# Post-norm decoder layer on one core: the mixer's GpSimd order, and the products ahead of its last mix

## The reference

```python
xn = _layernorm(x, ln_gamma, ln_beta)
k = jnp.einsum('btc,dc->btd', xn, Wk)
v = jnp.einsum('btc,dc->btd', xn, Wv)
r = jnp.einsum('btc,dc->btd', xn, Wr)
kv = k * v
weighted_kv = kv * jnp.power(td[None, None, :], t_idx)
csum = jnp.cumsum(weighted_kv, axis=1)
shifted = concatenate([zeros, csum[:, :-1]], axis=1)
wkv = tf * kv + td * shifted
out = jnp.einsum('btc,dc->btd', jax.nn.sigmoid(r) * wkv, Wo)
x = _layernorm(x + out)
```

## Time and profile before

| | |
|---|---|
| median of 3 runs | 2131.97 us (2131.47 to 2137.92) |
| profiled execution | 2134.5 us, its span 2132.7 us |
| granted TensorE clock, mean | 0.975 of full speed |
| TensorE busy | 1984.1 us, 93% |
| VectorE busy | 1530.2 us, 72% |
| ScalarE busy | 1254.4 us, 59% |
| GpSimd busy | 1478.0 us, 69% |
| mixer, 14.0 to 268.7 us | TensorE busy 226.12, VectorE 205.69, GpSimd 146.75, ScalarE 131.58 us; clock 0.99 |

### The profile page before, as it was taken

One profiled execution on the slowest core, in us unless ns is written; L12 is line 12 of the kernel. 1 busy time (PEld: TensorE's weight loads), 2 busy tenths in 40 slices (PEclk: granted clock), 3 DMA queues, 4 the chain that ended last, 5 costly groups with the idle time before them and its releaser, 6 DMA issues. The chain is left out here.

```text
span 2132.7 us, 51909 instructions
## 1 busy us (share of the span) xinstructions
PE 1984.1 (93%) x14320; PEld 1787.2 (84%) x14320; DVE 1530.2 (72%) x3648; ACT 1254.4 (59%) x3478; POOL 1478.0 (69%) x1691
## 2 busy tenths in 40 slices
PE   5999879999999999785999999999999999489997
PEld 5777668888887888675999999999999999468886
DVE  5888747777787788763777778888888888335554
ACT  3555446666666666532777777777777777224443
POOL 3656512777677677663677778888888888459764
PEclk9999999999999999997999999999999999789999
DMA  3300022432422423304666766777777777367542
GB/s 122 109 0 0 0 94 80 139 101 79 158 79 90 147 79 118 110 21 139 228 230 228 232 228 227 236 237 237 237 235 229 230 233 234 110 242 241 182 168 99
DMA packets 244904, 329.89 MB, mean 155 GB/s; under 512 B 50074, under 2 KB 167234, under 8 KB 244836
## 3 DMA queue, kind: packets, MB, share of 16 engines
q1 hardware_dynamic: 218788, 279.97, 40.5%
q0 software_dynamic: 26048, 49.10, 6.3%
HBM read 236.17 MB, written 77.18 MB: 147 GB/s over the span
## 5 line engine op out<-in xcount | busy, mean ns | idle before, releaser
L1336 POOL DMA_INDIRECT slot_token<-a_entry,a_slot_i x256 | 261.4, 1021 | 113.2 <-issue 71.8
L1818 POOL DMA_INDIRECT part_rows<-e_out,e_dest x184 | 211.0, 1147 | 74.2 <-issue 65.9
L1951 ACT ACTIVATE e_sg<-e_g 128x256 f32<-128x256 f32 x368 | 141.8, 385 | 204.7 <-PE e_g L1643 204.7
L1810 POOL DMA_INDIRECT e_xg<-x_rows,e_tok x188 | 196.5, 1045 | 85.1 <-issue 56.3
L2000 DVE TENSOR_TENSOR e_h<-e_sg,e_u 128x256 f32<-128x256 f32 x368 | 158.0, 429 | 100.4 <-PE e_u L1643 40.5
L1161 ACT ACTIVATE a_prob<-a_s,a_ntop 128x128 f32<-128x128 f32 x512 | 180.8, 398 | 3.0 <-DVE a_ntop L1515 2.9
L1826 POOL TENSOR_TENSOR e_wd1l<-e_raw_d,e_wd1h 128x256 fp32r<-128x256 f32 x184 | 145.5, 825 | 19.1 <-ACT e_wd1h L1931 18.4
L1826 POOL TENSOR_TENSOR e_wd0l<-e_raw_d,e_wd0h 128x256 fp32r<-128x256 f32 x184 | 145.9, 827 | 14.4 <-ACT e_wd0h L1931 13.6
L2015 DVE TENSOR_SCALAR e_out<-e_d,e_dest 128x256 f32<-128x256 f32 x184 | 80.6, 480 | 103.1 <-PE e_d L1643 103.1
L1643 PE MATMUL e_d<-e_wd1h,e_ht1h 128*128 128x256 f32 x368 | 109.4, 297 | 24.6 <-issue 24.6
L1023 PE MATMUL a_o<-a_wo,a_ot 128*128 128x256 f32 x512 | 123.1, 384 | 8.2 <-DVE a_ot L1582 8.2
(11 more groups left out here) (398 smaller groups left out, 7603.2 us busy)
## 6 DMA issues: line engine op xcount, KB each, us to landing
e_raw_g<-in_eg SPq DMA_DIRECT2D x94, 512.0 KB
e_raw_u<-in_eu SPq DMA_DIRECT2D x94, 512.0 KB, 5.6
e_raw_d<-in_ed SPq DMA_DIRECT2D x93, 512.0 KB
part_rows<-a_zero SPq DMA_DIRECT2D x16, 2048.0 KB
f_part<-part_rows SPq DMA_DIRECT2D x16, 2048.0 KB, 9.5
x<-in_x SPq DMA_DIRECT2D x16, 512.0 KB, 3.7
x_rows<-x SPq DMA_DIRECT2D x16, 512.0 KB
out_rows<-f_res SPq DMA_DIRECT2D x16, 512.0 KB, 10.2
```

The source lines that it names most:

```text
L1336: pool.indirect_dma_start(k.slot_tok, bass.IndirectOffsetOnAxis(ap=slot_i[:, j, q:q + 1], axis=0), entry[:, j, q, :], None, bounds_check=S ...
L1810: pool.indirect_dma_start(xg[a][:, n, :], None, k.x2_d, bass.IndirectOffsetOnAxis(ap=tok[a][:, n, 0:1], axis=0))\
L1818: pool.indirect_dma_start(k.part_d, bass.IndirectOffsetOnAxis(ap=dest[a][:, n, 1:2], axis=0), out[a][:, n, :], None).then_inc(put[a], 16)
L1951: act.activation(sg[m % 2][:], bank_g[m % 2][:, 0:SETW], ACT.Silu).then_inc(sg_rdy, 1)
```

## The change

GpSimd's period puts the root behind both wkv_in, in every period, and the context's low part between the two wkv_in of the last period. At the mixer's end TensorE makes four products ahead of the last mix instead of two, and ScalarE empties all four banks before the outgoing norm of group 14.

```diff
                 periods(pe, period)
-                project_ahead(range(2))
+                project_ahead(range(4))
                 mix(NG - 1, 1, 0)
                 mix(NG - 1, 1, 1)
-                project_ahead(range(2, 8))
+                project_ahead(range(4, 8))
...
                 periods(act, period)
-                empty_ahead(range(2))
+                empty_ahead(range(4))
                 norm_out(NG - 2)
-                empty_ahead((2, 3, 6, 7))
+                empty_ahead((6, 7))
                 norm_out(NG - 1)
...
                 def period(g, par):
                     decayed(g, 0)
-                    root(g + 2, 0 if more(g, 2) else TG, 2 * TG if at_least(g, 2) else TG)
                     if not more(g):
                         context_low()
                     decayed(g, 1)
+                    root(g + 2, 0 if more(g, 2) else TG, 2 * TG if at_least(g, 2) else TG)
                     gated(g, par, 0)
                     gated(g, par, 1)
```

## The result

| | before | after |
|---|---|---|
| median | 2132.76 us (4 runs, 2131.47 to 2137.92) | 2155.48 us (4 runs, 2151.46 to 2158.31) |
| ratio of the runs | | 1.0099, 95% interval 1.0082 to 1.0115 |
| span of the profiled execution | 2132.7 us | 2156.5 us |
| mixer's last instruction ends | 268.6 us | 289.0 us |

What follows compares the result with a forecast made beforehand. VectorE and GpSimd's 14.14 us ring was taken to bound the mixer. The root's new ring would make it 17.1 us late at period 15; less 0.3 at the end, 2131.97 + 16.8 = 2149 us, range 2142 to 2155.

Steps and rivals of the forecast that it cites:

- The ring with the root: Mixer loop: m_kv, wkv_in, root, m_xn, norms, m_kc, next m_kv would set the period, 15.41 us instead of 14.14.
- its slack: Kernel before, each period: m_kc ends at 82.70, m_kv needing it starts at 85.56, so 2.86 us spare.
- Rival A: Mixer loop: the stall goes, nothing replaces it, TensorE's 13.07 us decides; 14 us less, 2118; chance 0.05.
- Periods 0 to 3: Mixer's start, four-column roots and no norm of x in periods 0 and 1: period 3 begins 3.4 us late.
- Eleven periods at 1.27 us: Mixer loop, periods 3 to 14: each 1.27 us longer, making it 17.4 us late at period 14.
- TensorE's clock: Mixer loop: pauses of about 2 us could slow TensorE's products, up to 0.2 a period, 3 us in all.
- Period 14: Four-column root and only four norms: 12.80 us against 13.07, so 17.1 us late at period 15.
- The end: Mixer's tail: mix 0.8 to 2.0 us later, 2.0 given back; -0.3 taken, bounds -2 to +1.
- part 2 of the change: Last period, context's low part ahead of wkv_in and root: some 3 us earlier relative to m_kv, alone gives nothing.
- The port: VectorE and GpSimd's shared SBUF port: m_ve first in each period would shorten the ring by 0.17 us, 2147 us.

Runs made afterwards that it cites:

- e3: Changed kernel with ScalarE's m_xn behind the first m_kc, the outgoing norm ahead of the second gate, periods 0 to 3 written out: 2121.04 us, 0.9938 of before.
- e4: Kernel before with only ScalarE's norms reordered around m_kc, periods 0 to 3 written out, GpSimd's order and the end kept: 2133.3 us, ratio 1.0.
- e10: Kernel before with six idle 128x128 ScalarE instructions ahead of m_xn in periods 0 to 13, 2.33 us a period: 2136.16 us, ratio 1.0007.
- e11: Kernel before with twelve idle 128x64 ScalarE instructions ahead of m_xn in periods 0 to 13, 3.97 us a period: 2151.17 us, ratio 1.0075.
- e9: Changed kernel with TensorE's pauses in periods 2 to 14 filled by unused products, four ahead of the transpose, five ahead of the second half: 2156.12 us, single run.
- e2_tail: Kernel before with GpSimd's new order in period 15 alone and the new end: 2135.62 us, ratio 1.0009.
- e1: Changed kernel with GpSimd's new order kept and TensorE's and ScalarE's old end restored: 2157.7 us, 1.0116 of the kernel before.
- e6: Changed kernel with three idle 128x256 ScalarE copies ahead of m_xn in periods 0 to 13: 2175.53 us, 1.018 of the kernel before.

## Why the prediction held, and where it was short

- **The ring with the root**: right. 15.41 us were summed; the periods at full clock are 15.38 and 15.57. e3 and e4 show that the ring goes through ScalarE's norms, e10 and e11 that its slack was between 2.33 and 3.97, and e11's period puts it at 2.80. Rival A (2118) described what happens once that ring is opened too: e3 gave 2121.0.
- **Periods 0 to 3**: 3.4 were forecast, 3.1 came (74.53 against 71.40).
- **Eleven periods at 1.27 us, 14.0 in all**: mis-sized, 16.0 came. TensorE's clock was lower in part of them, which I had allowed for with up to 3 us and not put into the sum; e9 puts it at 1.2. The rest is the 0.19 us of every other period: I had taken m_kv to wkv_in as 0.83 and m_kc to m_kv as 0.71 in all of them.
- **Period 14**: -0.3 forecast, -0.5 came (12.55 us).
- **The end: -0.3 forecast, +1.8 came** (30.43 us from the last first m_kv to the end, against 28.65). This is the term that failed. I had the mix 0.8 to 2.0 us later; it came 2.9 later, 16.93 us behind m_kv. The second m_kv came 7.05 us after the first and not 5.9 (258.57 to 265.62), and wkv_in (2.20 us beside VectorE's wg_l, which I had allowed for; 2.28 before), the root and both m_y stand behind it. What made it late is part 2 of the change, which I had costed at nothing: the context's low part now runs on GpSimd beside VectorE's own low parts, ahead of the second m_kv. VectorE before and after, and GpSimd after:

```profile
240.63 2.36 DVE L565 TENSOR_TENSOR wu_both<-k,wu_both 128x512 fp32r<-128x512 f32 x2
```

```profile
259.50 3.44 DVE L565 TENSOR_TENSOR wu_both<-k,wu_both 128x512 fp32r<-128x512 f32 x2 [0.19 <-ACT wu_both L392]
```

```profile
260.65 1.75 POOL L495 TENSOR_TENSOR a_ct<-ctx_raw,a_ct 128x512 fp32r<-128x512 f32 x1
```

  That is 1.08 of the 1.34 us by which this step grew (7.05 against 5.71). e2_tail, with the old order up to the last period, has the same effect one instruction later: its VectorE's a_ct takes 1.65 us instead of 0.69, and the step is 6.67 us. And behind a pause of 4.52 us the mix took 6.34 us, where I had left it its old 5.16; the last norm started 11.4 us after it and not 10.5:

```profile
275.50 6.34 PE L347 MATMUL m_o<-m_wo,m_y 128*128 128x256 f32 x16 [4.52 <-POOL m_y L511]
```

- **The place of the rest**: 3.13 + 16.0 - 0.5 + 1.8 = 20.4 us in the mixer. The stages behind it took 1867.5 us in the changed kernel's profile and 1864.1 before, and from 1858.9 (e1) to 1867.8 (e6) in the ten others. I read these 3.4 us as scatter of single executions: they are less than the 8.9 between those ten, and nothing in the change reaches there. They are not shown to be it.
- **The port**: the rule of the Trainium skill's page "SBUF — State Buffer" (section on SBUF's two sides), an exclusive lock for whoever comes first, could have given a shorter ring if GpSimd had won. In all 16 periods VectorE's scan was first, by 0.05 to 0.06 us, and m_ve took 1.20 to 1.22, so no run shows the other order.

## What to carry to other kernels

A visible wait is worth what the next ring leaves of it. Before a step is moved behind a wait, follow what reads its result, in order, until the chain comes back to the step: the shift less the slack at the last join is the price; here that was 4.07 - 2.80 = 1.27 us a period, and the periods at full clock grew by 1.24 and 1.43 in turn. When an edit only hands the stall on, look for its partner: the root's move alone cost 1%, the norms' move alone gave nothing, and together they gave 13 us. Here the in-order engine had to get the urgent small work (m_kc) ahead of work whose input is late. And an instruction that is moved without a gain is not free: the context's low part, moved ahead, held up VectorE by 1 us.

## What the runs showed of the hardware

- TensorE's granted clock fell to its lower level behind two pauses of 0.90 and 1.37 us with 1.1 us of transposes between, in some periods and not in others of the same shape (0.90 of full speed in the window from 89.90, 1.00 in the one behind the pauses of 0.91 and 1.38 us at 118.91 and 121.38); I had taken from a pause of 2.35 us at 247.44 in the kernel before that such ones are harmless. With 0.94 us more in each period (e6) the granted clock was 0.84 in every second period from period 8 on, which was 1.5 us longer for it, beside the 0.19 above.
- A ScalarE copy of 128x256 took 0.31 us from start to start, the same with scale and offset per partition 0.49, and 128x64 with them 0.33.
